# Expert weights split in the first stage and kept on chip; per tile VectorE copies both parts

## The reference, cut to what matters

```python
x = x + L0_gnn(layernorm(x), adj)       # 5 groups of nodes, two graph convolutions each (128->256->128), relu
x = x + L0_ffn(layernorm(x))            # 8 experts 128->512->128, the two best of 8 for each token
x = x + L1_gnn(layernorm(x), adj, mask) # one graph convolution over all 128 nodes, relu
x = x + L1_ffn(layernorm(x))            # shared 3-layer net plus the two best of 4 small experts

# L0_ffn, for each of the 8 experts e:
h = relu(einsum('bsd,hd->bsh', x, W1[e]) + b1[e])
y = einsum('bsh,dh->bsd', h, W2[e]) + b2[e]
out = out + combine[..., e:e + 1] * y
```

## Time and profile before

| | us |
|---|---|
| median of 3 runs | 1252.68 (1250.98 to 1254.02) |
| the profiled execution | 1253.57 |
| its span, first to last instruction | 1251.8 |

### The profile page before, as it was taken

How to read it: one execution, slowest core, us unless ns; L and a number is a source line. 1 busy time by engine, 2 the same in 40 slices (tenths; PEclk the granted TensorE clock), 3 DMA queues, 4 the chain that set the end, 5 groups by cost and what they waited for, 6 DMA issues and landing times. The chain is left out here.

```text
span 1251.8 us, 20777 instructions
## 1 busy us (share of the span) xinstructions
PE 1143.5 (91%) x6346; PEld 856.7 (68%) x6346; DVE 1060.6 (85%) x3170; ACT 949.8 (76%) x1885; POOL 735.5 (59%) x678
## 2 busy tenths in 40 slices
PE   6889979459999999999999981899999999999998
PEld 4667756327788888888888861566667666666675
DVE  4678987897999999999999975688888888888875
ACT  3448765448999999999999971687787877877874
POOL 3346555636666666655666617776677766777720
PEclk9999985559999999999999995899999999999999
DMA  5579764502323333322333542223222232222310
GB/s 196 195 221 293 228 196 143 200 21 74 83 81 76 84 83 85 83 78 79 83 85 85 72 64 70 58 76 85 69 72 73 70 88 72 70 73 72 81 37 26
DMA packets 136466, 124.51 MB, mean 99 GB/s; under 512 B 14591, under 2 KB 116067, under 8 KB 135204
## 3 DMA queue, kind: packets, MB, share of 16 engines
q1 hardware_dynamic: 119075, 87.77, 22.8%
q0 software_dynamic: 17280, 35.42, 13.2%
HBM read 83.64 MB, written 39.50 MB: 98 GB/s over the span
## 5 line engine op out<-in xcount | busy, mean ns | idle before, releaser
L1081 POOL DMA_INDIRECT exg<-xln_scratch,ids x284 | 279.5, 984 | 190.9 <-PE p_ex L1134 105.4
L1380 POOL DMA_INDIRECT yg<-expert_rows_scratch,pos_i x256 | 254.5, 994 | 97.1 <-issue 72.7
L1102 ACT ACTIVATE ehr<-p_eh,bc 128x512 f32<-128x512 f32 x284 | 195.2, 687 | 22.7 <-DVE ehl L1222 19.2
L1222 DVE TENSOR_TENSOR ehl<-ehr,ehh 128x512 fp32r<-128x512 f32 x284 | 191.4, 691 | 7.0 <-ACT ehh L1105 6.8
L1105 ACT ACTIVATE ehh<-ehr 128x512 fp32r<-128x512 f32 x284 | 179.6, 633 | 9.0
L1138 PE MATMUL p_eh<-exh,wh 128*128 128x512 f32 x284 | 124.6, 439 | 0.8 <-ACT exh L1096 0.8
L1150 PE MATMUL p_ey<-ehl,wh 128*128 128x512 f32 x284 | 116.8, 411 | 0.0
L1387 POOL TENSOR_TENSOR root_l<-pre_l,mhalf 128x4 f32<-128x4 f32 x64 | 66.5, 1039 | 80.1 <-DVE pre_l L1654 79.2
L1142 PE MATMUL p_eh<-exl,wh 128*128 128x512 f32 x284 | 112.1, 395 | 0.0
L1139 PE MATMUL p_eh<-exh,wl 128*128 128x512 f32 x284 | 112.0, 394 | 0.0
L1147 PE MATMUL p_ey<-ehh,wh 128*128 128x512 f32 x284 | 112.0, 394 | 0.1
(11 more groups left out here) (226 smaller groups left out, 2912.4 us busy)
## 6 DMA issues: line engine op xcount, KB each, us to landing
expert_rows_scratch<-eyo SPq DMA_DIRECT2D x71, 256.0 KB, 2.3
xtok<-in_x_tok SPq DMA_DIRECT2D x8, 1024.0 KB, 7.3
an<-in_a_t SPq DMA_DIRECT2D x16, 512.0 KB, 4.7
xln_scratch<-xl SPq DMA_DIRECT2D x16, 512.0 KB, 4.4
at<-in_a_t SPq DMA_DIRECT2D x32, 256.0 KB, 3.0
out<-outx SPq DMA_DIRECT2D x32, 256.0 KB, 2.6
wj<-in_w_grp SPq DMA_DIRECT2D x16, 321.0 KB, 4.8
exg<-xln_scratch,ids POOLq DMA_INDIRECT x284, 2.6
```

Source lines behind the costliest of these rows:

```text
L1081: pool.indirect_dma_start(out=xg[p][:, k, :], out_offset=None, in_=xln_d, in_offset=bass.IndirectOffsetOnAxis(ap=ids[:, R * j + k:R * j + ...
L1102: nc.scalar.activation(hr[c % 2][:, :], p_h[c][:, :], ACT.Relu, bias=bc[p][:, c:c + 1])\
L1222: nc.vector.tensor_tensor(hl[:, c, :], hr[c % 2][:, :], hh[:, c, :].bitcast(F32), ALU.subtract)\
L1380: pool.indirect_dma_start(out=yg[p][:, c, k, :], out_offset=None, in_=y_d, in_offset=bass.IndirectOffsetOnAxis(ap=pos_i[:, c, R * j + k:R ...
```

## The change

- The eight experts' weights are loaded in the first stage, one expert a turn (turns 2 to 9, 0.5 MB each), at the end of SyncE's turn.
- In turns 3 to 10 ScalarE rounds one expert's 128x1024 weights to `whi`, between `xs` and `ht`. In turns 4 to 11 VectorE subtracts `whi` from the weights, in place (`wlo` is the memory of `wall`), right behind `ys`.
- In the expert stage `take` copies the tile's slices of `whi` and `wlo` to `wh` and `wl`, with no wait between the two copies.
- To make room: packed adjacencies are loaded straight into `ag` (five buffers, was four, and `ar` is gone), the relu is done in place in `os` (VectorE now waits for the store, ScalarE no longer), `degrees` adds two halves of 128x512 after each other into a `dsum` of half the size, the masks are float16, two unused constants go, and the last stage's constants are loaded in the expert stage behind the second store. `he` of the last stage lies in `whi`.

```diff
-GA = 4
+GA = 5
@@ first stage, SyncE
                     def load(j):
                         sp.dma_start(xg[j % 2][:, :, :], x_grp[item[j]]).then_inc(loaded[j % 2], 16)
-                        sp.dma_start(ar[j % 2][:, :, :], a_grp[item[j]]).then_inc(loaded[j % 2], 16)
+                        if j >= GA:
+                            sp.wait_ge(o_done, j - GA + 1)
+                        sp.dma_start(ag[j % GA][:, :, :], a_grp[item[j]]).then_inc(loaded[j % 2], 16)
...
+                        if W0 <= t < W0 + E0:
+                            sp.dma_start(wall[:, t - W0, :], w_exp[:, t - W0, :]).then_inc(w_loaded[(t - W0) % 4], 16)
@@ first stage, GpSimd
-                        pool.wait_ge(deg_ready, b + 1)
-                        nc.gpsimd.tensor_tensor(dsum[:, :, :], dsum[:, :, :], an[b % 2][:, :, :], ALU.add)\
-                          .then_inc(deg_ready, 1)
+                        for h in range(2):
+                            pool.wait_ge(deg_ready, 2 * b + h + 1)
+                            nc.gpsimd.tensor_tensor(dsum[:, :, :], dsum[:, :, :], an[b % 2][:, h * R:h * R + R, :],
+                                                    ALU.add).then_inc(deg_ready, 1)
@@ first stage, ScalarE
                             last.then_inc(xs_ready, 1)
+                        if W0 < t <= W0 + E0:
+                            e = t - W0 - 1
+                            act.wait_ge(w_loaded[e % 4], 16 * (e // 4) + 16)
+                            nc.scalar.activation(whi[:, e, :], wall[:, e, 0:WW], ACT.Copy).then_inc(whi_ready, 1)
...
                             act.wait_ge(os_ready, t)
-                            act.wait_ge(rows_stored[p], 16 * (t // 2) - 15)
-                            nc.scalar.activation(orl[p][:, :, :], os_[p][:, :, :], ACT.Relu).then_inc(orl_ready, 1)
+                            nc.scalar.activation(os_[p][:, :, :], os_[p][:, :, :], ACT.Relu).then_inc(orl_ready, 1)
@@ first stage, VectorE, behind ys
+                        if W0 + 1 < t <= W0 + 1 + E0:
+                            e = t - W0 - 2
+                            dve.wait_ge(whi_ready, e + 1)
+                            nc.vector.tensor_tensor(wlo[:, e, :], wall[:, e, 0:WW], whi[:, e, :].bitcast(F32),
+                                                    ALU.subtract).then_inc(wlo_ready, 1)
@@ expert stage, VectorE
-                    def take(j, p, w, half, ready):
+                    def take(p, e, half, ready):
                         cols = slice(half * H0, (half + 1) * H0)
-                        nc.vector.tensor_copy(wh[p][:, cols], w[:, cols]).then_inc(wh_ready, 1)
-                        dve.wait_ge(wh_ready, 2 * j + half + 1)
-                        nc.vector.tensor_tensor(wl[p][:, cols], w[:, cols], wh[p][:, cols].bitcast(F32),
-                                                ALU.subtract).then_inc(ready, 1)
+                        for dst, src in ((wh, whi), (wl, wlo)):
+                            last = nc.vector.tensor_copy(dst[p][:, cols], src[:, bass.ds(e, 1), cols]
+                                                         .rearrange("p a w -> p (a w)"))
+                        last.then_inc(ready, 1)
```

More of the change, by code:

```diff
@@ L177, in build @@
         wall = alloc(top, "wall", [P, E0, EW])
[L178 to L190, removed]
+        whi = alloc(top, "whi", [P, E0, WW], F32R)
+        wlo = wall[:, :, 0:WW].bitcast(F32R)
         lc_loaded = sem("l_consts_loaded")
@@ L204, in build @@
         an_loaded = pair("r_an_loaded")
-        w_loaded = sem("w_loaded")
+        w_loaded = [sem(f"w_loaded{k}") for k in range(4)]
+        whi_ready = sem("w_high_ready")
+        wlo_ready = sem("w_low_ready")
+        W0 = 2
         with ExitStack() as ctx:
@@ L335, in store @@
                         sp.wait_ge(orl_ready, j + 1)
-                        sp.dma_start(dst, orl[j % 2][0:rows, :, :]).then_inc(rows_stored[j % 2], 16)
+                        sp.dma_start(dst, os_[j % 2][0:rows, :, :]).then_inc(rows_stored[j % 2], 16)
                     def load_rows(i):
@@ L445, in _ @@
                             roots(b)
[L446 to L450, removed]
+                    pool.wait_ge(deg_ready, 2 * NB + 1)
+                    nc.gpsimd.tensor_tensor(dsum[:, 0:2, :], dsum[:, 0:2, :], dsum[:, 2:4, :], ALU.add)\
+                      .then_inc(deg_ready, 1)
+                    pool.wait_ge(deg_ready, 2 * NB + 2)
                     nc.gpsimd.tensor_tensor(deg[:, :], dsum[:, 0, :], dsum[:, 1, :], ALU.add).then_inc(deg_ready, 1)
-                    pool.wait_ge(deg_ready, NB + 4)
+                    pool.wait_ge(deg_ready, 2 * NB + 3)
                 @block.scalar
@@ L1023, in build @@
         lgp.close()
+        prob = alloc(top, "prob", [P, 2, B])
+        texp = alloc(top, "texp", [P, NTP], I32)
+        wgcn = alloc(top, "wgcn", [P, D])
+        bgcn = alloc(top, "bgcn", [P, D])
+        maskt = alloc(top, "maskt", [P, B])
+        ws = alloc(top, "ws", [P, 3 * P])
+        bs = alloc(top, "bs", [P, 2])
+        w1 = alloc(top, "w1", [P, E1, P])
+        w2 = alloc(top, "w2", [P, E1, P // 2])
+        w3 = alloc(top, "w3", [P, 2, D])
+        be = alloc(top, "be", [P, E1 + 2])
+        vraw = alloc(top, "vraw", [KV, R, D])
+        gws = alloc(top, "gws", [P, E1])
+        gbs = alloc(top, "gbs", [P, E1])
+        selraw = alloc(top, "selraw", [2 * R * E1, R, 2, P])
         with ExitStack() as ctx:
@@ L1068, in _, with l_constants @@
                 def _(sp):
-                    dst = y_d.rearrange("(t p) d -> p t d", p=P)
+                    rows = y_d.rearrange("(t p) d -> p t d", p=P)
+                    def l_constants():
+                        for dst, src in ((wgcn[:, :], w_gcn), (bgcn[:, :], b_gcn), (maskt[:, :], mask_t),
+                                         (ws[:, :], w_s), (bs[:, :], b_s), (w1[:, :, :], e_w1), (w2[:, :, :], e_w2),
+                                         (w3[:, :, :], e_w3), (be[:, :], b_e), (vraw[:, :, :], b_out),
+                                         (gws[:, :], gw), (gbs[:, :], gb), (selraw[:, :, :, :], selp_d)):
+                            sp.dma_start(dst, src).then_inc(lc_loaded, 16)
                     for j in range(NTP):
@@ L1245, in turn @@
                         if after and before:
-                            take(j + 1, q, w, 1, w2_ready)
+                            take(q, e, 1, w2_ready)
                         h_lo(j, 3)
@@ L1251, in _ @@
                     for t in range(2):
-                        w = of_tile(t)
-                        take_1(t, t, w)
-                        take(t, t, w, 1, w2_ready)
+                        e = of_tile(t)
+                        take_1(t, e)
+                        take(t, e, 1, w2_ready)
                     nc.vector.tensor_scalar(prob[:, 1, :], dif[:, :], 1.0, None, ALU.add).then_inc(set_, 1)
@@ L1295, in build @@
             hs = [alloc(ctx, f"hs{k}", [P, W]) for k in range(2)]
-            he = [alloc(ctx, f"he{e}", [P, W]) for e in range(E1)]
+            he = [whi[:, e, 0:W].bitcast(F32) for e in range(E1)]
             rp = [alloc(ctx, f"rp{k}", [P, W]) for k in range(2)]
```

49 lines of the change are left out of this document (17 added, 32 removed).

## The result

| | before | after |
|---|---|---|
| median of the runs, us | 1253.51 (1250.98 to 1255.49, 7 runs) | 1257.46 (1254.76 to 1258.64, 7 runs) |
| profiled execution / its span, us | 1253.57 / 1251.8 | 1255.35 / 1253.5 |
| mean granted clock of PE | 0.938 | 0.941 |
| last `p_eyo` transposes begin, us | 746.03 | 747.42 |
| routing stage begins (`dis_g`), us | 235.12 | 242.14 |

The ratio after / before is 1.0028, 95% interval 1.0017 to 1.0039: slower by 2.1 to 4.9 us. The forecast was 2.5 us slower. In the table routing begins 7.0 us later, and the last tile's output transposes only 1.4 us later: 5.6 us came back between the two.

What follows compares the result with a forecast made beforehand. PE, DVE and ACT were near full in the expert stage; in the first, `dinv`, held by GpSimd's add, lay on the path. Terms -5.6 + 5.4 + 0 + 1.0 + 1.7 = +2.5 us gave 1255.2, range 1246 to 1261.

Steps and rivals of the forecast that it cites:

- the likeliest case: Whole kernel: the summed forecast holds, with a time of 1252 to 1258 us; chance 0.40.
- Take becomes two copies: Expert stage: two copies replace cast and subtraction, a tile falls from 6.49 to 6.40 us; 5.6 us gained.
- rival 1: Expert stage: all 15.7 us that PE's weight load waits for `ehl` come back, total 1245; chance 0.13.
- Subtraction: First stage, behind `ys`: VectorE's new operation puts off GpSimd's add, so `dinv`, `xsb`, `zs` and PE move by 0.85 us.
- Rival 2: `ys` to `dinv`, turns 4 to 8: the add is not put off, the subtraction costs nothing; total 1248, chance 0.17.
- rival 3: First stage: `root`, then the add, holds the subtraction, `dinv` ends 1.6 us later a turn; total 1260, chance 0.17.
- Turns 4 to 8: First stage: five turns, each 0.85 us longer through the put-off add, +4.3 us in all.
- Turn 10: First stage: `os` waits only 1.17 us, from `zs` on, so the subtraction costs +1.1 us.
- turns 9 and 11: First stage: `os` waits 3.34 and 2.62 us for PE, so the 1.2 us subtraction fits and costs 0.
- Rounding: Turns 3 to 10: ScalarE's 1.0 us copy fits its 1.08 us of idle time between `xs` and `ht`; 0.
- Loads: Turns 2 to 9: weight loads delay the next turn's rows, in turns 7 to 9; +1 us, from 0 to 4.9.
- Degrees: Turns 10 to 15: two half adds take 0.28 us more, `pre` and `root` wait; +1.7 us, from 0 to 3.

Runs made afterwards that it cites:

- The experiment: The kernel before with GpSimd's degrees added in two halves of 128x512 instead of one of 128x1024, nothing else changed: 1252.96 us, ratio 1.0004 (0.9991 to 1.0016).

## Why the prediction came out right

The sign and the likeliest case were right: +2.5 forecast, +3.5 measured (2.1 to 4.9). The mechanism of both main terms held, and the agreement of the sum is in part luck: the term of turns 4 to 8 was too small by 3.5 us, and a stretch that the change hardly touches happened to be 3.6 us shorter. Step by step:

- *Take becomes two copies, -5.6.* Right in size: 1.4 - 7.0 = -5.6 in these two executions, and 65 tiles at 0.08 us make 5.2. Taking the starts of matmuls rather than the wait of a weight load (15.7 us) decided this; rival 1 would have needed tiles below 6.3. The reason given was half of it. The forecast named both the 0.47 us a tile and the waits for itself, and leaned on the first; either was enough.
- *Subtraction, +0.85 a turn.* 0.89 measured. Its route was right (subtraction, add, `dinv`), its make-up was not: not the whole from a late add, but 0.62 from the add and 0.27 from `wdi` and `b2w`. And the add didn't start with the end of the subtraction, as the forecast's sign had it, but before it, and took longer. Rivals 2 and 3 are out: at full clock a turn is 9.03, where 8.1 would have been the one and 9.7 the other. (Rival 2 was also priced too well: its sum of -4.6 leaves out the 1.7 of the degrees and the 1.1 of turn 10, which it gives no reason to drop.) `root`, the start of rival 3, held nothing: the subtraction began at 61.76 while `root` ran to 62.24, and took its plain 1.22 us.
- *Turns 4 to 8, +4.3.* This term was too small. By the starts of `root` they cost 7.76 us: 5 x 0.89 and 3.3 for the clock that fell in turns 5 and 6. The sum priced PE's longer wait at its length and not at what it does to PE's clock. Before, with 1.25 us of idle time, the clock was full from 60 to 80 us; with 2.15 it was not. The 3.3 is this execution's; with four turns at the lower clock, as in the kernel with the slow copy, it was 6.6.
- *Turn 10, +1.1, turns 9 and 11, 0.* Measured +1.65, -0.07, -0.15. But the 1.65 isn't the subtraction's: kernels with no subtraction there took 10.95 to 10.98 us for turn 10, and the changed one 11.24. So its own part is 0.3 at most. That this term came out near its number is luck.
- *Rounding, 0.* In turn 4 it runs from 46.63 to 47.67, and `ht` follows at 47.80 with no idle time: the cover was exact, as said. In turn 6 `ht` waits 1.75 us, for PE at the lower clock.
- *Loads, +1.0.* Not in turns 7 to 9 but before turn 4: turns 1 and 2 are longer by 0.87 and 1.02, turn 3 is shorter by 0.82, and `root` of turn 0 begins 0.64 later: 1.7 in all. Nor is that shown to be the loads: the same sum is 1.0 with the halves alone, which loads no weights, and from 0.2 to 1.7 in other kernels with the loads.
- *Degrees, +1.7.* Turns 11 to 14 are 0.4 us shorter in sum than before; what turn 10 has from the halves is open. The row behind the term was read too simply: `pre` does take 0.74 us, as forecast, but in turn 11 what `root` waits for is the next `pre`, and that waits for PE's `p_thin`:

```profile
110.10 0.74 DVE L649 TENSOR_SCALAR pre<-st 128x4 f32<-128x4 f32 x1
...
111.80 0.16 DVE L651 TENSOR_SCALAR nz<-p_thin 128x4 f32<-128x4 f32 x1 [0.96 <-PE p_thin L520]
```

The 0.96 us of idle time hides the 0.26. The experiment leaves up to 2 us.

The starts of `root` differ by 10.7 us at turn 15, more than the 8.1 that the forecast had there, and yet routing begins 7.0 later and not 10.7. In the stretch to which the change brings nothing but the halves of the degrees, from that `root` to `dis_g`, the kernel before took 90.35 us and the kernel after 86.69. The granted clock of 150 to 195 and of 195 to 240 us was 0.82 and 0.54 in the one, 0.93 and 0.61 in the other. Across the profiles of this study that stretch took 86.0 to 91.9 us, with and without the change. So over 3 us of the agreement at the start of routing is these two executions' own; what caused the clock there isn't shown.

## What to carry to other kernels

A short instruction that VectorE has time for still costs what it does to the others: look at what the neighbour engine starts in that stretch, at what stood in the shade of a held instruction, and at whether what follows in the same engine's order is on the path. Moving the neighbour away doesn't mend the last; moving the instruction does. Before adding work, look for tiny operations with a long duration (`dinv`, 1.15 us for four numbers): they mark a collision that a wait on the other engine can move away, here 0.9 us a turn. When a wait of PE grows in a stage at full clock, price the clock as well, with a spread, for it fell in two to four turns of the same program; and measure lateness by the starts of matmuls, not by the waits of weight loads.

## What the runs showed of the hardware

- A GpSimd add that VectorE's two-input subtraction holds does not show as idle: its duration grows. In turns 4, 5 and 6 of the changed kernel it started 0.61, 0.78 and 0.44 us after the subtraction and took 1.73, 1.56 and 1.89 us instead of 1.27, and each time it ended 1.11 or 1.12 us after the subtraction's end. In the earlier trace rows the delay had shown as idle time instead.
- A VectorE instruction with one input tensor was held by that add just as `dinv` was: `wdi`, 128x4, took 1.24 us (0.23 alone). Yet the one-input statistics did not hold the add. The Trainium skill (SBUF — State Buffer, Who interferes with whom) counts `tensor_scalar` among the operations that can take the pair of ports shared with GpSimd, and says that other instructions with one SBUF input do not contend; both runs agree.
- Copies from float32r to float32r of 128x512 took 443 ns on VectorE, the maximum with two inputs of the same size 679.
- GpSimd's gather instruction grew longer where VectorE's two operations of a take follow each other without a wait. Groups of that instruction from 310 to 740 us, of the kernel before, the kernel after, the one with the slow second copy (no wait either), and the one with the wait kept between the copies:

```profile
L1081 POOL DMA_INDIRECT exg<-xln_scratch,ids x258 | 254.1, 985 | 163.3 <-PE p_ex L1134 103.3 <-issue 60.1
```

```profile
L1091 POOL DMA_INDIRECT exg<-xln_scratch,ids x262 | 279.3, 1066 | 139.0 <-PE p_ex L1144 77.1 <-issue 61.9
```

```profile
L1091 POOL DMA_INDIRECT exg<-xln_scratch,ids x267 | 282.1, 1056 | 148.9 <-PE p_ex L1144 82.5 <-issue 64.3 <-remote 2.1
```

```profile
L1093 POOL DMA_INDIRECT exg<-xln_scratch,ids x262 | 248.5, 948 | 169.5 <-PE p_ex L1146 108.6 <-issue 60.9
```

  It cost nothing, for GpSimd had that slack waiting for `p_ex`; why the wait between the copies brings it down to 948 ns wasn't tried.
- The clock of PE fell to 1.2 GHz in eight of the twelve turns 4 to 7, over three executions, in which PE had waited 2.15 us for `zs`, and in none of the four where useless transposes had cut that wait to 0.85 us.
